# Macaron transformer block on one core: the last front's layer norm from GpSimd to the vector engine and ScalarE, router logits computed by expert, a batch half's projections moved from the first feed-forward pass into the attention's opening

## The reference, cut to what matters

```python
x = x + 0.5 * ffn(layernorm(x))
x = x + attn(layernorm(x))          # 16 heads of 8, 3D rope, biases
x = x + 0.5 * ffn(layernorm(x))

def ffn(x):                          # expert choice routing, E = 8 experts
    logits = einsum('bsd,ed->bse', x, gate_w)
    affinity = softmax(logits, axis=-1)                 # over the experts
    gating, idx = top_k(affinity.T, k=256)              # each expert picks 256 tokens per batch
    h = silu(x[idx] @ w_gate.T) * (x[idx] @ w_up.T)     # inner width 512
    out[idx] += gating * (h @ w_down.T)
```

## Time and profile before

| | us |
|---|---|
| median of 3 runs | 1208.99 (1207.38 to 1209.43) |
| the profiled execution | 1207.35 |
| its span, first to last instruction | 1205.3 |
| first layer's iterations | from 68.6 to 297.4 |
| window | 299.0 to 363.0 |
| attention and its tail | 363 to 971 |
| second layer's iterations, to the last scatter's issue | 971 to 1198.5 |
| of these, it 19 starts on PE | 1020.3 |

### The profile page before, as it was taken

The page is one execution under the profiler, slowest core; times in us unless marked ns, Lnnn a source line. Parts: engine busy times, 40 slices in busy tenths (PEclk is TensorE's granted clock), DMA queues, the critical chain, the costliest instruction groups (busy, mean ns, idle before and its releaser), DMA issues.

```text
span 1205.3 us, 23761 instructions
## 1 busy us (share of the span) xinstructions
PE 1088.2 (90%) x8900; PEld 478.3 (40%) x8900; DVE 918.8 (76%) x1510; ACT 769.6 (64%) x1461; POOL 600.1 (50%) x619
## 2 busy tenths in 40 slices
PE   6199999898599999999999999999998889999993
PEld 6167666565132222222222222222222256666762
DVE  5745855465979999999999999999997554854441
ACT  3054322432368999999989999899999836222220
POOL 4046888775378511100003447455430187677886
PEclk6579999999598999999999999999999988999997
DMA  9025456458514220212111222112310125345553
GB/s 274 32 60 115 91 112 136 88 118 198 135 37 123 61 64 19 58 46 58 40 29 40 52 52 62 25 40 58 81 45 8 31 79 130 83 92 101 114 101 30
DMA packets 93065, 93.95 MB, mean 78 GB/s; under 512 B 14684, under 2 KB 70108, under 8 KB 92920
## 3 DMA queue, kind: packets, MB, share of 16 engines
q1 hardware_dynamic: 70424, 75.66, 22.6%
q0 software_dynamic: 22528, 16.79, 10.3%
HBM read 64.22 MB, written 30.13 MB: 78 GB/s over the span
## 4 chain that ended last, share of the span: by engine, by line
DVE 43%; PE 35%; issue 11%; POOL 5%; ACT 4%; DMA 1%; SPq 0%; DVEq 0%; POOLq 0%; another core or an unknown queue 0%; ACTq 0%
DVE mx L1877 38%; PE pA L1329 7%; PE pS L1317 7%; POOL out_dram L655 3%; ACT Pt L1154 3%; PE pO L1318 3%; PE pS L1318 3%; PE pO L1469 3%; DVE ge L1564 2%; PE pS L1490 2%; PE pA L1297 2%; PE pS L1235 2%; POOL xg L632 1%; PE pA L1405 1%; PE pA L1235 1%
## 5 line engine op out<-in xcount | busy, mean ns | idle before, releaser
L1877 DVE TENSOR_REDUCE mx<-pA 128x2 f32<-128x1024 f32 x512 | 585.2, 1217 | 13.8 <-PE pA L1405 13.0
L1154 ACT ACTIVATE Pt<-pS 128x512 f32<-128x512 f32 x1024 | 556.3, 596 | 30.9 <-PE pS L1490 25.0
L1469 PE MATMUL pO<-Pt,Vst 128*16 128x256 f32 x4096 | 321.5, 386 | 12.5 <-ACT U L1145 12.5
L1049 ACT ACTIVATE Pt<-pS 128x512 f32<-128x512 f32 x128 | 76.4, 597 | 199.9 <-PE pS L1317 176.6
L632 POOL DMA_INDIRECT xg<-zd,idx x128 | 128.4, 1003 | 149.4 <-DVE idx L1684 76.3
L1405 PE MATMUL pA<-Kst,Qst 48*128 48x512 bf16 x704 | 140.9, 397 | 20.1 <-DVE mx L1877 18.9
L1469 PEld LDWEIGHTS pO<-Pt,Vst 128*16 128x16 f32 x4096 | 68.0, 94 | 204.3 <-issue 107.2
L1317 PE MATMUL pS<-Pt,wg 128*128 128x512 f32 x256 | 139.7, 628 | 4.5 <-DVE Pt L1711 2.1
L1490 PE MATMUL pS<-Qst,Kst 51*128 51x512 bf16 x704 | 138.6, 390 | 5.1 <-issue 1.0
L722 POOL TENSOR_TENSOR mparts<-mx,onesm 128x32 bf16<-128x32 f32 x16 | 4.0, 252 | 267.1 <-DVE mx L1882 210.9
L1329 PEld LDWEIGHTS pA<-wd,Pt 128*128 128x128 f32 x960 | 113.5, 192 | 16.8 <-issue 16.8
(11 more groups left out here) (229 smaller groups left out, 1214.7 us busy)
## 6 DMA issues: line engine op xcount, KB each, us to landing
wg<-w_gate_dram SPq DMA_DIRECT2D x32, 256.0 KB
wu<-w_up_dram SPq DMA_DIRECT2D x32, 256.0 KB
wd<-w_down_dram SPq DMA_DIRECT2D x32, 256.0 KB
qk<-parts SPq DMA_DIRECT2D x64, 96.0 KB
Kst<-qk SPq DMA_DIRECT2D x132, 32.0 KB
zd<-Z SPq DMA_DIRECT2D x8, 512.0 KB
vp<-pair SPq DMA_DIRECT2D x4, 1024.0 KB, 4.6
Vst<-vp SPq DMA_DIRECT2D x16, 256.0 KB
```

What stands on the lines that cost most here:

```text
L1049: S.activation(sg[:, u % 2, :], pG[u % 2], ACT.Silu).then_inc(s_silu, 1)
L1154: S.activation(Pt[:, s % 4, j, r * 512:(r + 1) * 512], pS[:, bank_of(k, 4 * s + 2 * j + r), :], ACT.Exp, scale=SCALE).then_inc(s_exp, 1)
L1469: last = M.matmul(pO[32 * h:32 * h + 16, cols], Vst[k][:, s % 8, h, :], Pt[:, s % 4, h // 2, (h % 2) * 512 + 256 * a:(h % 2) * 512 + 256 * ...
L1877: V.reduce_max(mx2[:, k, 2 * j:2 * j + 2, c, half], pA[ring[q, a] % 2][:, :, :], AX.X).then_inc(s_Ar, 1)
```

## The change

- Layer norm 10 leaves POOL. DVE computes its moments in slot (16,0), where the selection masks of it 18 (all_onehots(18), before ahead of it 16) now stand too; ACT takes both square roots in (17,3), DVE both scale-and-shifts in (17,4), ACT normalises batch 2 in (17,4) and (18,0), batch 3 in (18,1) and (18,2).
- The attention's last output projection moves from (16,2) and (16,4) to (16,4) and (17,1). Front 3's steps 0 to 3 go to (18,0) to (18,3), 4 and 5 to (19,0) and (19,1), 6 to 8 to (19,2) to (19,4), and 9 to 18 to all five slots of it 20 and 21 (four each before). The last two stay in it 22.
- Fronts 1 and 3: logits with the gate as the stationary operand, padded to 32 columns, in four column groups; ACT copies the bank out; four transposes bring tokens back onto partitions.
- u = 2 and 3 (batch 1's projections) leave it 14 and 15 for the window, behind pieces 0 to 13; rope and the split go to POOL and ACT with them, ahead of what was there.
- eps becomes a bias of the square root, and the addition veps on DVE goes.
- SP: store_values(0) behind load_weights(15), store_values(1) behind the loads of x, load_weights(18) ahead of write_out(3).

```diff
+    place[1, 4] = ("g", 1)
-    for m in range(5, 25):
+    for m in range(5, 15):
         place[divmod(55 + m, 5)] = ("s", m)
-    place[16, 2], place[16, 4] = ("p", 3, 0), ("p", 3, 1)
-    for n, at in enumerate([(17, 3), (17, 4), (18, 0), (18, 1), (18, 2), (18, 4)] + [(19, k) for k in range(5)] +
-                           [(it, k) for it in (20, 21) for k in range(4)] + [(22, 0), (22, 1)]):
+    place[16, 4], place[17, 1] = ("p", 3, 0), ("p", 3, 1)
+    for n, at in enumerate([(18, 0), (18, 1), (18, 2), (18, 3), (19, 0), (19, 1)] + [(19, k) for k in range(2, 5)] +
+                           [(it, k) for it in (20, 21) for k in range(5)] + [(22, 0), (22, 1)]):
         place[at] = ("f", 3, n)
+    place[18, 4] = ("g", 3)
...
-    for u, at in ((4, 22), (5, 28), (6, 32), (7, 37)):
-        for i in range(4):
-            window[divmod(at + i, 32)] = ("PR", u, i)
+    for u, ats in ((2, (0, 2, 4, 6)), (3, (8, 10, 12, 13)), (4, range(22, 26)), (5, range(28, 32)), (6, range(32, 36)), (7, range(37, 41))):
+        for i, at in enumerate(ats):
+            window[divmod(at, 32)] = ("PR", u, i)
...
@@ SyncE
-            store_values(0)
             store_parts(0)
             load_weights(15)
+            store_values(0)
             store_parts(1)
             load(0)
             load(1)
-            store_values(1)
             load_weights(16)
             load_weights(17)
             for b in range(2, B):
                 sp.wait_ge(s_scat[b], 256)
                 load_x(b, x1_in)
+            store_values(1)
...
             write_out(2)
+            load_weights(18)
             write_out(3)
-            load_weights(18)
             store_z(10)
             store_z(11)
@@ GpSimd
             scatter(RUN - 1)
+            product(2, 0)
+            product(2, 1)
+            add_products(2)
+            product(3, 0)
             rest(2)
+            product(3, 1)
+            add_products(3)
+            lowest(2)
             rest(3)
-            lowest(2)
             lowest(3)
...
-                if it == RUN:
-                    normalise_sums(10)
                 if it + 2 < NIT:
                     gather(it + 2)
-                if it == RUN:
-                    normalise_rows(10)
@@ ScalarE
-                S.activation(sd[:, tiles(i)], veps[:, tiles(i)], ACT.Sqrt).then_inc(s_sd, 1)
+                if i == 0:
+                    act.wait_ge(s_fill, 3)
+                S.activation(sd[:, tiles(i)], mv[:, tiles(i), 1], ACT.Sqrt, bias=eps[:, 0:1]).then_inc(s_sd, 1)
...
+                if key and key[0] == "g":
+                    act.wait_ge(*written(key))
+                    S.activation(by_expert, sidebank, ACT.Copy).then_inc(s_room, 1)
...
-                if (it, k) == (17, 1):
+                if (it, k) == (17, 3):
+                    deviation(10)
                     deviation(11)
-                if (it, k) == (17, 3):
+                if (it, k) == (17, 4):
+                    normalise(10, 0, 4)
+                if (it, k) == (18, 0):
+                    normalise(10, 4)
+                if (it, k) == (18, 1):
                     normalise(11, 0, 4)
-                if (it, k) == (17, 4):
+                if (it, k) == (18, 2):
                     normalise(11, 4)
...
-            middle(2)
-            middle(3)
...
+            for u in (2, 3):
+                for i in range(4):
+                    projected(u, i)
+                value_rows(u)
+            high(2)
             deviation(6)
+            middle(2)
             deviation(7)
             act.wait_ge(s_sd, 8)
             S.activation(warm[:, :], sd[:, 0:8], ACT.Exp)
             normalise(6)
+            high(3)
             turned_half(0)
             turned_half(1)
+            middle(3)
             normalise(7)
@@ TensorE
+            def logits_by_expert(hh):
+                bank, sem = open_bank(("g", hh))
+                pe.wait_ge(*was_read(("f", hh, 3)))
+                for g in range(4):
+                    last = M.matmul(bank[32 * g:32 * g + 32, :], gate_t[:, :], ZT[:, g * 512:(g + 1) * 512], start=True, stop=True,
+                                    tile_position=(0, 32 * g))
+                last.then_inc(sem, 1)
...
                     if hh:
-                        pe.wait_ge(*was_read(("f", hh, 3)))
...
+                        pe.wait_ge(*was_read(("g", hh)))
+                        for k in range(4):
+                            last = M.transpose(bank[:, k * P:(k + 1) * P], by_expert[:, k * P:(k + 1) * P], ident[:, :])
@@ VectorE
-                link(last)
-                V.tensor_scalar(veps[:, tiles(i)], mv[:, tiles(i), 1], EPS, None, ALU.add).then_inc(s_ve, 1)
+                last.then_inc(s_ve, 1)
...
                 if (it, k) == (16, 0):
+                    all_onehots(RUN + 2)
+                    moments(10)
+                if (it, k) == (16, 1):
                     invert_tail(1)
-                if (it, k) == (16, 1):
+                if (it, k) == (16, 2):
...
                     context(3, 0)
-                if (it, k) == (16, 3):
+                if (it, k) == (17, 0):
...
                     context(3, 1)
-                if (it, k) == (17, 0):
+                if (it, k) == (17, 2):
                     add_to_x(3, 1)
                     moments(11)
-                if (it, k) == (17, 2):
+                if (it, k) == (17, 4):
+                    scale_and_shift(10)
                     scale_and_shift(11)
...
-            all_onehots(RUN + 2)
```

74 lines of the change are left out of this document (43 added, 31 removed).

## The result

| | us |
|---|---|
| the changed kernel, median of 4 runs | 1198.07 (1196.67 to 1199.75) |
| the kernel before, median of 4 runs beside it | 1208.96 (1207.38 to 1209.43) |
| ratio | 0.9913, 95% interval 0.9896 to 0.9930 |
| profiled execution of the changed kernel | 1198.03, span 1196.2 (before: 1207.35, 1205.3) |

The change gains 10.9 us by the medians, 9.3 by the profiled executions; the forecast was 11.8. The median lies within 1 us of the forecast; several terms of the sum don't.

The account below looks back on a forecast made before the run. DVE's score maxima and PE share the chain of waits (43% and 35%), so time is saved only where either is last. Terms -0.6 - 1.5 - 9.7 + 0.5 + 1.5 - 2.0 = -11.8 took 1208.99 to 1197.2 us, range 1193 to 1202.

Parts of the forecast that it names:

- It 14 and 15: End of the first layer: eight projections, two sets of value rows and a wait of 1.07 leave PE, -9.7 us.
- Start and logits of front 1: First layer's start: veps additions leave DVE's chain, -0.6 us; four column-group matmuls replace sixteen small ones, -1.5 us.
- Rival D: Logits of fronts 1 and 3: column groups don't overlap, so that change does nothing; 1201 to 1204 us, chance 0.06.
- load(0): Start of the window: the load lands at 288 to 290, against pieces ready 9.7 us earlier; +0.5 us, ends 0 and +7.7.
- Rival B: Start of the window: load(0) becomes what starts it, at up to +7.7 us; up to 1204.4 us, chance 0.12.
- Window: Between the layer's end and the attention: moved projections mostly hidden, POOL and ACT barely in time; +1.5 us, ends 0 and +7.
- rival C: Window: moved projections aren't hidden at PE's lower clock, 20.2 us instead of 0.5; 1216.9 us, chance 0.09.
- It 16: Second layer: POOL's layer norm and PE's wait go, -5.2 us; masks and moments cost 0.9; -4.3 us in all.
- f(3,0): Front 3's first step in (18,0): PE waits for ACT's layer norms; +3.5 us, ends 0 and +7.
- Logits of front 3: Second layer: shorter logits save 2.7 us and the half clock behind them another 2.7; -5.4 us, ends -2 and -7.
- weights of it 19: Start of it 19: PE waits for weights that SP issues behind store_z(11); +1.5 us, ends 0 and +4.7.
- rival A: Second layer: neither layer norms nor weights of it 19 make PE wait, -7.0 us there; 1192.2 us, chance 0.2.

Follow-up runs that it names:

- u_logits: The changed kernel with the sixteen small matmuls for the logits of fronts 1 and 3 again; median 1210.58 us, 1.0012 of the kernel before.
- load_early: The changed kernel with lowest(1) one slot earlier and its write inside load_weights(15), ahead of store_values(0); median 1196.09 us, 0.9875 of the kernel before.
- all_three: The changed kernel with weights of it 19 ahead of both token writes, layer norm 10 normalised earlier, and load_early's edit; median 1189.63 us, 0.9820 of the kernel before.
- after_again: The changed kernel run once more without any edit, in the second set; median 1196.98 us, 0.9889 of the kernel before.
- logits_w19_first: The changed kernel with the old small logits matmuls of fronts 1 and 3 and weights of it 19 ahead of token writes; 1205.48 us, 0.9976 of the kernel before.

## Why the prediction was right, and where it was wrong

The forecast of 1197.2 was right, by its main term; that it came within 1 us of the median is luck: errors of over 3 us stand in the sum in both directions, and by the profiled executions it is 2.5 us off. By its steps:

- *It 14 and 15*, -9.7: -9.96, and undoing it returned exactly that. Eight PE halves of 0.86 and a wait of 1.07, each with a row, made the safest term the largest.
- *Start and logits of front 1*, -2.1: -4.0 up to idx 4. The logits were mis-sized: 2.5 (2.8 when undone), not 1.5. The 0.5 given back for DVE's chain wasn't lost, and the sum had nothing for the gap ahead of it 2's first product (0.46 before, 0.78 in u_logits) that the column groups fill. Rival D falls, since four column groups of 512 columns take 1.06. The start's -1.5 up to idx 3 isn't firm: after_again has idx 3 at 88.85, 0.3 later than before.
- *load(0)*, +0.5: +1.28, up to 4.8 in a variant. Rival B was right about the place. What was mis-sized is the way from the parts to the first piece: the last DMA was to go out 2 us earlier and went out 1.3 earlier against idx 15, since the parts' issues took longer, and it was to land in 2.5 us, for which no row stood, and PE started 3.6 behind it. That puts the first piece at the end of the forecast's "288 to 290", not at its start. The 1 MB of values held the load in load_early alone.
- *Window*, +1.5: +2.4. The size is near, the mechanism wrong. PE's clock held and the projections were hidden (rival C falls). deviation(7) was in time. The loss was mostly DVE's two shifts, beside POOL's operations, for which the sum had nothing.
- *It 16*, -4.3: -5.1, of which +0.6 is the price of masks and moments, forecast as 0.9. *f(3,0)*, +3.5: the wait was 3.36, but the half clock behind it made it 4.8, and taking it away gave 6.2 by the medians. *Search*, +2.7: +2.66.
- *Logits of front 3* -5.4 and *weights of it 19* +1.5: together -0.5, not -3.9. This is the term that failed. The logits' -5.4 was right (with the weights in time idx 20-21 is 15.26, 5.05 below before); the weights cost 4.0 to 4.55. I priced "a little over 1 us" of wait, from 3.5 us until PE is ready and 4.7 until the weights are through; it was 3.0 and 5.85 (1001.31 to 1004.31 and 1007.16), a wait of 2.85, and I had nothing for the half clock behind it, 1.7.
- The second layer up to idx 24 was +1.8 with it 16 counted from its start, not -2.0; rival A, that no new wait would show there, falls. With the orders of SP and ACT changed as well the forecast's gain would have been there (all_three is 7.4 us under after_again). That the end shifts one for one behind POOL's last wait was not quite so: +1.5 behind idx 25, covered by a half clock less.
- In the sum the 3.8 us by which the second layer fell short stand against 3.3 us by which the first layer up to idx 13 ran faster than forecast; 1.8 of these didn't come again. What is left between -11.8 and the profiled -9.0 (last outputs) is load(0) and window, 1.7 more than forecast, and the tail ahead of it 16, +1.0, which is not shown to be the change's; the rest is under 0.3 each.

## What to carry to other kernels

Price a new wait on PE with its clock: here the new waits of 2.4 to 3.7 us, at (18,0) and at it 19, ended in the half clock or had it right behind them in 13 of 17 cases, for 1.7 to some 7 us more, and not in the other four. So a wait and the work behind it are not two terms that add, and the same wait has two prices. When a step moves later, look at what else is queued behind its data on SP: a transfer needed soon (weights) belongs ahead of one needed later (tokens for it 24), and a wait belongs ahead of the one DMA that needs it, not ahead of all nineteen. Work moved into one engine's idle time can slow another engine's smallest instruction; look for small DVE instructions that read SBUF beside GpSimd's tensor operations, those with two SBUF inputs first.

## What the runs showed of the hardware

- A 128x8 SCALAR_TENSOR_TENSOR with both inputs in SBUF took 0.17 us with GpSimd idle and 0.97 to 0.99 and 1.14 to 1.15 beside GpSimd's TENSOR_TENSOR, in all ten executions without an edit there; held apart by one wait it was 0.17 again. It ended 0.02 to 0.03 us behind GpSimd's operation. DVE's maxima from PSUM (1.19 to 1.23 beside them and without them) and its layer-norm statistics weren't slowed beside the same operations. That is the lock of the Trainium skill's "SBUF — State Buffer" (SBUF: two separate sides): a DVE instruction with two SBUF inputs and a GpSimd instruction that reads SBUF exclude each other for the whole instruction. The trace agrees, to the end time.
- Two SBUF inputs are not needed. The CAST that writes the index has one; it takes 0.17 us, and 1.59 and 0.91 in it 16 and 17 of the kernel before, beside the layer norm on GpSimd, each time ending 0.02 us behind GpSimd's operation (DVE's timeline, then POOL's):

```profile
978.86 1.59 DVE L1684 CAST idx<-row 128x4 int32<-128x4 f32 x1
```

```profile
978.21 2.22 POOL L765 TENSOR_TENSOR sin<-Z 128x1024 f32<-128x1024 f32 x1
```

- In front 3, sixteen float32 products with 8 moving columns twice saw the granted clock fall from 1.00 to its lower level while PE was busy without a gap (before and logits_w19_first), and the product behind them took 2.05 and 2.06 instead of 1.02 to 1.13; in front 1 the clock held in all three executions. Behind four column groups with 512 moving columns it held wherever no wait followed.
- The same first layer took 15.2 to 20.7 us between idx 12 and 13. In the longest, GpSimd reached a gather 6.4 us after its index was ready, PE waited 2.77 for it and 3.77 for ACT further on (2.43 in the shortest), with a half clock behind. A difference of one profile there says nothing of a change.
